# A gated recurrent scan on one core: low halves from a scan instruction, 48-column tiles in runs of 12, and block work in halves

## The reference, cut to what matters

```
xz = seq @ W_z ; xr = seq @ W_r ; xh = seq @ W          # for all steps at once
def step(h, xs):
    z  = sigmoid(xzt + h @ U_z + vz)
    r  = sigmoid(xrt + h @ U_r + vr)
    hh = tanh(xht + r * h @ U + vh)
    h_new = (1.0 - z) * h + z * hh
    return (h_new, h_new)
_, out_t = jax.lax.scan(step, h0, xs)
```

## Time and profile before

| | us |
|---|---|
| median of 3 runs | 6808.79 (6806.77 to 6811.7) |
| the profiled execution's own time | 6811.76 |
| its span | 6809.9 |
| PE busy in the span | 5998.4 (88%) |
| PEld busy | 5642.2 (83%) |
| DVE busy | 4955.6 (73%) |
| ACT busy | 3331.6 (49%) |

### The profile page before, as it was taken

How to read it: one execution, slowest core, us unless ns; L and a number is a source line. 1 busy time by engine, 2 the same in 40 slices (tenths; PEclk the granted TensorE clock), 3 DMA queues, 4 the chain that set the end, 5 groups by cost and what they waited for, 6 DMA issues and landing times.

```text
span 6809.9 us, 488240 instructions
## 1 busy us (share of the span) xinstructions
PE 5998.4 (88%) x200232; PEld 5642.2 (83%) x200232; DVE 4955.6 (73%) x43503; ACT 3331.6 (49%) x22603; POOL 3.5 (0%) x13
## 2 busy tenths in 40 slices
PE   7888888888888888888888888888888888888888
PEld 7888888888888888888888888888888888888888
DVE  5777777777777777777777777777777777777777
ACT  3444444444444444444444444444444444444444
POOL 0000000000000000000000000000000000000000
PEclk8999999999999999999999999999999999999999
DMA  2000000000000000000000000000000000000000
GB/s 84 17 18 15 18 17 18 17 17 17 18 17 18 15 18 17 18 18 15 18 17 18 17 18 15 18 17 18 17 17 17 18 17 18 15 18 18 17 18 15
DMA packets 80315, 129.97 MB, mean 19 GB/s; under 512 B 12336, under 2 KB 18480, under 8 KB 80304
## 3 DMA queue, kind: packets, MB, share of 16 engines
q1 hardware_dynamic: 80304, 129.81, 5.5%
HBM read 20.46 MB, written 8.65 MB: 4 GB/s over the span
## 4 chain that ended last, share of the span: by engine, by line
PE 71%; DVE 26%; issue 3%; SPq 0%; DMA 0%; ACT 0%; ACTq 0%; DVEq 0%
PE pair_r L252 30%; PE ps_z L252 24%; PE pair_h L252 17%; DVE pair_h L487 8%; DVE h_part L522 5%; DVE h_part L541 4%; DVE h_part L527 2%; DVE keep L523 2%; DVE zn L536 2%; DVE h_part L532 2%; PE ps_z L212 0%; DMA u_raw<-in_L_cond_U 0%; PE ps_o L212 0%; DVE u_max L424 0%; PE ps_x L224 0%
## 5 line engine op out<-in xcount | busy, mean ns | idle before, releaser
L252 PEld LDWEIGHTS pair_r<-h_part,u_part 128*128 128x128 f16 x65536 | 1845.1, 96 | 1119.9 <-DVE h_part L541 1115.8
L252 PE MATMUL pair_r<-h_part,u_part 128*128 128x32 f16 x65536 | 2048.7, 177 | 771.1 <-DVE h_part L541 758.6
L252 PE MATMUL pair_h<-rh_part,u_part 128*128 128x32 f16 x65536 | 2016.6, 177 | 12.5 <-DVE rh_part L505 12.5
L252 PE MATMUL ps_z<-h_part,u_part 128*128 128x32 f16 x65536 | 1961.5, 176 | 0.0
L252 PEld LDWEIGHTS pair_h<-rh_part,u_part 128*128 128x128 f16 x65536 | 1842.8, 96 | 17.3 <-DVE rh_part L505 15.7
L252 PEld LDWEIGHTS ps_z<-h_part,u_part 128*128 128x128 f16 x65536 | 1795.3, 95 | 0.0
L487 DVE TENSOR_REDUCE pair_r<-pair_r 128x4 f32<-128x20 f32 x4096 | 759.4, 186 | 818.1 <-PE pair_r L252 615.1
L351 ACT ACTIVATE pair_r<-pair_r 128x4 f32<-128x4 f32 x4096 | 644.8, 158 | 1445.1 <-DVE pair_r L487 1182.4
L487 DVE TENSOR_REDUCE pair_h<-pair_h 128x4 f32<-128x12 f32 x4096 | 717.7, 175 | 665.7 <-PE pair_h L252 665.7
L351 ACT ACTIVATE th_z<-ps_z 128x8 f32<-128x8 f32 x2048 | 364.1, 178 | 1046.0 <-DVE ps_z L487 1046.0
L337 ACT ACTIVATE pair_h<-xp 128x8 f32 (+1 forms) x2049 | 369.9, 181 | 807.8 <-DVE zn L536 807.8
(11 more groups left out here) (70 smaller groups left out, 3275.9 us busy)
## 6 DMA issues: line engine op xcount, KB each, us to landing
w_stage<-w_in SPq DMA_DIRECT2D x384, 256.0 KB, 2.3
x_tok<-in_x SPq DMA_DIRECT2D x68, 128.0 KB, 2.6
out_dram<-o_tok SPq DMA_DIRECT2D x66, 128.0 KB, 2.3
mlp_w<-in_L_cond_W SPq DMA_DIRECT2D x2, 1024.0 KB, 6.9
u_raw<-in_L_cond_U_r SPq DMA_DIRECT2D x1, 1024.0 KB, 5.6
u_raw<-in_L_cond_U_z SPq DMA_DIRECT2D x1, 1024.0 KB, 7.6
u_raw<-in_L_cond_U SPq DMA_DIRECT2D x1, 1024.0 KB, 10.3
w_in<-in_L_cond_W_r SPq DMA_DIRECT2D x4, 256.0 KB, 9.8
```

What stands on the lines that cost most here:

```text
L252: last = nc.tensor.matmul(bank[:, SLOT * m:SLOT * m + WIDE].rearrange("p (r n) -> p r n", n=n), u_part[:, g, part, k, gm * P:(gm + 1) * P] ...
```

## The change

1. **Low parts from a scan.** `gated_full` and `new_full` for each half are gone. The low part now comes from one `tensor_tensor_scan` over 12 places (4 channels-and-batch entries of 3 places, `STEP` = 3). In each entry the scan multiplies by the factors in the places (zero, tanh, h or z_mul) and subtracts what stands in the high part's places (-1, -1, high for r; -1, 0, high for h), so the third place is the product less its high part. The tanh results are therefore written by ACT into SBUF tiles `r_scan` and `n_scan`, h lives in `r_scan` and z_mul in `n_scan`, all with a stride of 3 elements. The low part waits for the high part (`rhi`, `nhi`). `zn` is made once, 8 wide, after the last low part, and h waits for it.
2. **Runs of 12 places.** A matmul streams 48 columns rather than 32: runs of 12 f16 places taken from `h_part` or `rh_part`, with two places of each run that matter. The reduces read columns that are 12 apart.
3. **Order on PE.** In the r group 14 matmuls rather than 12 stand ahead of the wait for half 1, so output half 0 is complete after 22 rather than 20. The h group stays at 12 and 20.
4. **Block work.** `make_out`, `make_y` and the copy to `y_cur` are each cut into two halves and put behind different turn steps; `hist` is laid out with time innermost; the output transposes move from turn step 1 to 2, the output copy from 2 to 3. The projection's store moves from DVE to ACT, as one 64-wide instruction before the tanhs of the fifth step and one behind its `hist` copy. SP issues the store of the output after the twelve weight loads of a block rather than before.
5. `seed(pair_h)` no longer waits for `zn1`. GpSimd has some more memsets at the start.

```
-    WIDE = 32
-    SLOT = WIDE + B
+    STEP, RUN, WIDE = 3, 12, 48
+    SLOT = WIDE + RUN
+    PITCH = HS * STEP + RUN - B * STEP
...
-                n = (ADDENDS[g] - 1) * B
-                moving = parts[:, k, :, :].rearrange("p a b -> p (a b)").unsqueeze(1).broadcast_to([P, WIDE // n, n])
+                n = ADDENDS[g] - 1
+                at = k // HC * n * PITCH + k % HC * B * STEP
+                runs = parts[:, at:at + n * PITCH].rearrange("p (a c) -> p a c", c=PITCH)[:, :, 0:RUN]
+                moving = runs.unsqueeze(1).broadcast_to([P, WIDE // (n * RUN), n, RUN])
...
+                ahead = 3 if g == R else 2
...
+                for m, k in first[:ahead]:
+                    product(1, m, k)
                 pe.wait_ge(s[src + "1"], t1)
...
-                        tanh(ps_r[hf][:, TANH:TANH + HS], ps_r[hf], R, HS, f"r{hf}_sum", t1, f"r{hf}_th")
+                        tanh(r_scan[:, half[hf], 1], ps_r[hf], R, HS, f"r{hf}_sum", t1, f"r{hf}_th")
...
+                def low(parts, count, hi, hf, factors, done):
+                    V.tensor_tensor_scan(part_of(parts, count, hf, hi + 1), factors[:, half[hf]].rearrange("p s c -> p (s c)"),
+                                         part_of(parts, count, hf, hi), 0.0, ALU.mult, ALU.subtract).then_inc(s[done], 1)
...
-                new_full(0)
                 keep_low()
                 new_low(0)
                 new_high(1)
-                new_full(1)
                 new_low(1)
-                V.tensor_tensor(h_cur[:, :], keep[:, :], zn[:, :], ALU.add).then_inc(s["h_ok"], 1)
+                V.tensor_tensor(zn[:, :], z_mul, n_scan[:, :, 1], ALU.mult).then_inc(s["zn_ok"], 1)
+                dve.wait_ge(s["zn_ok"], t1)
+                V.tensor_tensor(h_cur, keep[:, :], zn[:, :], ALU.add).then_inc(s["h_ok"], 1)
...
+            def store_projection(i, ring, bb):
+                return A(xp[:, i, bass.ds(ring, TB), bb], ps_p[:, bb * TB:(bb + 1) * TB], ACT.Identity,
+                         bias=v_bias[:, i, bb:bb + 1])
...
-                    if proj is not None and u == K - 1:
-                        store_projection(*proj)
-                    if turn is not None and u == 0:
-                        make_out(turn[0])
-                    if turn is not None and u == 2:
-                        dve.wait_ge(s["y_copied"], turn[1])
-                        make_y(turn[2])
+                    if turn is not None and u < 2:
+                        make_out(u, turn[0])
+                    if turn is not None and u >= 2:
+                        make_y(u - 2, turn[2], turn[1])
```

More of the change, by code:

```diff
@@ L121, in gru_kernel, with part_of, place, keep_place @@
         half = (slice(0, HS), slice(HS, S))
+        by_half = lambda a: a.rearrange("p (h s) -> p h s", h=2)
+        def part_of(parts, count, hf, part):
+            at = (hf * count + part) * PITCH
+            return parts[:, at:at + HS * STEP]
+        def place(parts, count, hf, part, step=STEP - 1):
+            return part_of(parts, count, hf, part).rearrange("p (s c) -> p s c", c=STEP)[:, :, step]
+        def keep_place(low):
+            both = h_part[:, 0:2 * 2 * PARTS * PITCH].rearrange("p (h a s c) -> p h a s c", h=2, a=2 * PARTS, c=STEP)
+            return both[:, :, KEEP + low, 0:HS, STEP - 1]
         BYTES = 16 * B
@@ L303, in steps @@
                         transpose_block(ps_x, lambda c: x_tok[:, c * P:(c + 1) * P]).then_inc(s["x_tr"], 1)
-                    if turn is not None and u == 1:
+                    if turn is not None and u == 2:
                         put_out(turn[1])
             def put_out(nb):
-                pe.wait_ge(s["o_sum"], nb)
+                pe.wait_ge(s["o_sum"], nb * 2 if isinstance(nb, int) else pe.snap(nb * 2))
                 transpose_block(ps_o, lambda c: oT[:, c * B:(c + 1) * B, :].rearrange("p b t -> p (b t)"))\
@@ L351, in tanh, with steps @@
                 A(to, bank[:, SUM:SUM + n], ACT.Tanh, scale=scale_reg[g]).then_inc(s[done], 1)
-            def steps(t0, count, ring, turn=None):
+            def store_projection(i, ring, bb):
+                return A(xp[:, i, bass.ds(ring, TB), bb], ps_p[:, bb * TB:(bb + 1) * TB], ACT.Identity,
+                         bias=v_bias[:, i, bb:bb + 1])
+            def steps(t0, count, ring, turn=None, proj=None):
                 for u in range(count):
                     t1 = act.snap(t0 + (u + 1))
+                    if proj is not None and u == K:
+                        act.wait_ge(s["proj_mm"], act.snap(proj[2] + 2))
+                        store_projection(proj[0], proj[1], 0)
                     prv = act.snap(ring + (u - 1) if u else (ring + (2 * TB - 1)) % (2 * TB))
@@ L570, in steps, with make_out @@
+            def make_out(part, ring):
+                V.scalar_tensor_tensor(oT[:, half[part], :], hist[:, half[part], bass.ds(ring, TB)], 1.0 / H_SCALE,
+                                       y_cur[:, half[part], :], ALU.mult, ALU.add).then_inc(s["o_sum"], 1)
+            def steps(t0, count, turn=None):
                 for u in range(count):
                     step(dve.snap(t0 + (u + 1)))
-                    if proj is not None and u == K - 1:
-                        store_projection(*proj)
@@ L574, in steps @@
[L574 to L579 removed]
+                    if turn is not None and u < 2:
+                        make_out(u, turn[0])
+                    if turn is not None and u >= 2:
+                        make_y(u - 2, turn[2], turn[1])
             with dve.Fori(0, NB) as n:
                 other = dve.snap(((n + 1) % 2) * TB)
[L583 removed]
+                steps(dve.snap(n * TB), TURN, turn=(other, n, dve.snap(n + 2)))
@@ L584, in _ @@
                 with dve.Fori(0, GM) as i:
-                    steps(dve.snap(n * TB + i * BODY + TURN), BODY, proj=(dve.snap(n * GM + i + 2), i, other))
+                    steps(dve.snap(n * TB + i * BODY + TURN), BODY)
             dve.wait_ge(s["copied"], 1)
-            make_out((NB - 1) % 2 * TB)
+            for part in range(2):
+                make_out(part, (NB - 1) % 2 * TB)
 _INS = ["x", "cond_1024", "L0_cond_W1", "L0_cond_b1", "L0_cond_W2", "L0_cond_b2",
```

153 lines of the change are left out of this document (73 added, 80 removed).

## The result

The changed kernel takes 6748.12 us (median of 4 runs, 6746.14 to 6750.98), against 6808.76 us for the kernel before beside it (4 runs). The ratio is 0.9911, 95% interval 0.9895 to 0.9926. It is faster by 0.9%, 61 us, where 116 us were forecast.

What follows compares the result with a forecast made beforehand. A ring through PE and DVE was taken to bound the kernel. Span 6809.9 less 72 (steps), 31 (store) and 15 (turn), plus 2, gave 6694 us, so a median of 6693; range 6630 to 6800.

Steps and rivals of the forecast that it cites:

- plain steps: Every step of the ring through PE and DVE: 0.035 us saved, 72 us over 2048 steps.
- fifth steps: Last step of a round: moving the projection's store off DVE saves a further 0.08 us, 31 us in all.
- turn: Four steps with block work: halved output block and the like save 0.46 us a block, 15 us in all.
- the r part's rival: r's chain misses its tie with z's end by 0.05 us, steps save nothing: 6765 us, chance 0.12.
- round steps all alike: Sign of being right: the five steps of a round take equal time.
- the waits of the h group on the scan of r: Sign of being wrong: new waits of PE's h group for r's scan.
- The step that failed: Late h priced only at half output blocks behind it: four cost 0.03 to 0.07 us each, 0.2 a block.
- scan and dependence save 0.042: Behind the h group: low part freed from the full product saves 0.06 us, the longer scan costs 0.018.
- all else costs 0.007: Per step: h's half 0 starts its high part 0.002 us later, and the r part's tie costs 0.005.
- half-throughput rule: DVE's built-in scan runs at half throughput: 0.021 us longer instead of 0.018, so a step gains 0.003 less.
- 0.007 for the end of the last matmul of a group: On PE, 16 more columns delay the end of a group's last matmul by 0.007 us; PE's pace is unchanged.
- The rival that 48 columns set PE's pace: Every matmul slows, at 1.5 ns each by 295 us: about 6988 us, chance 0.07.
- the rival of a dearer scan: DVE's scan takes 215 ns rather than about 180, in the h and r parts: about 6903 us, chance 0.11.

Runs made afterwards that it cites:

- zn_early: The changed kernel with zn moved ahead of the second scan of h; 6663.31 us, ratio 0.9787.
- h_late: The kernel before with one more dependent DVE instruction, a copy of zn, ahead of h; 7040.86 us, ratio 1.0343.
- h_late48: The kernel h_late with 48 columns in each matmul rather than 32; 7021.82 us, ratio 1.0325.
- pairs: The changed kernel with two rounds written out per loop pass on PE, ACT and DVE; 7842.05 us, ratio 1.1513.
- dve_pairs: The changed kernel with two rounds written out per loop pass on DVE alone; 6868.77 us, ratio 1.0102.
- no_scan: zn_early with the scan replaced by full products and four-element differences, the new layout kept; 6971.96 us, ratio 1.0242.
- wide48: The kernel before with 48 columns in each matmul rather than 32; 6831.01 us, ratio 1.0035.
- ahead3: The kernel before with 14 r matmuls rather than 12 ahead of the wait for half 1; 6827.79 us, ratio 1.0039.
- act_store: The kernel before with the projection's store moved from DVE to ACT, placed as in the change; 6791.62 us, ratio 0.9981.

## Why the prediction was half right

The sum against the measurement, in us a block (36 plain steps, 12 fifth, 12 first, 4 of the turn), each place as the difference to before:

| place | forecast | after | zn_early |
|---|---|---|---|
| plain steps | 36 x -0.035 = -1.26 | 36 x -0.046 = -1.66 | -1.70 |
| fifth steps | 12 x -0.115 = -1.38 | 12 x -0.118 = -1.42 | -1.42 |
| first steps | 12 x -0.035 = -0.42 | 12 x +0.123 = +1.48 | -0.58 |
| turn | 4 x -0.035 - 0.46 = -0.60 | -0.35 | -0.86 |
| block | -3.66 | -1.95 | -4.54 |

Times 32, the forecast is 117 us and the measurement 62, as between the spans 6809.9 and 6748.3.

The 6748 us lie within the range, but that is luck in part: the range reached so far for the sake of the r part's rival, and what used that room is a cost to which the prediction gave no term. Its own sign "round steps all alike" is the one that failed, and of its signs of being wrong the waits of the h group on the scan of r came, in the long first steps.

**The step that failed** is that of the turn: "the last scan starts at 3.28 in the step, zn at 3.38 and h, which waits for zn, at 3.57". The number is right (h at 0.35 to 0.40 behind the r group's start; 3.57 is 0.35 into the next step). But the lateness was priced only where block work stands behind h. DVE has one more thing there: at the end of each round it goes back to the head of its loop, and 0.55 us lie between h and the next reduce. Before, h started 0.19 after the r group and the loop's instructions 0.06 ahead of h, so the way back was hidden, with some 0.06 over up to the 0.74 at which the reduce is due. After, 0.39 + 0.55 is 0.94. Against the forecast that is (0.123 + 0.035) x 12 x 32 = 61 us in the rounds, and 0.25 x 32 = 8 in the turns, where the larger gain in the block work (below) made up for a part. Three sides show it: zn_early takes the lateness out of the change, h_late and h_late48 put it into the kernel before, and pairs and dve_pairs have long and usual first steps in one execution, with and without the way back. The plain steps gave back 13 us of this loss, 0.046 each instead of 0.035.

**The h stretch and the scan.** The net was right and its parts were not. Forecast: scan and dependence save 0.042, all else costs 0.007. In the new layout, no_scan puts the scan at 0.15, and the rest of the layout at 0.10. Of that, wide48 measured 0.014 for columns and ahead3 0.015 for the order. That leaves some 0.07 for the tanhs to SBUF and for operands at a stride of three elements; the order of DVE's instructions is the same in both. The rows show that each is dearer in no_scan than before: a tanh 176 ns against 158, the high part of h 165 against 153, the four-element difference 171 against 163. How much each adds to the step stays open. By the half-throughput rule that the prediction takes from the Trainium skill ("DVE: opcode table, instruction layouts, handler registers and perf-mode slots", Datapath and trigger behaviour) the scan would be 0.021 us longer than a four-element difference. The trace does not settle it: 183 ns is 0.020 more than the difference of the kernel before (L541, 163), but 0.012 more than the one in the new layout (171).

**48 columns.** The term "0.007 for the end of the last matmul of a group" came out twice as large in wide48, 0.014 us a step, 22 us in all. The rival that 48 columns set PE's pace is refuted: z's 32 loads take 0.81 us in wide48, and r's take 0.79 after the change. At 1.2 GHz they do count. The first step of the changed kernel (window: us, PE, PEld, DVE and ACT busy, clock):

```profile
75.43:79.24 3.81, 3.81 (x96) 3.81 (x97) 1.38 (x10) 1.12 (x8) 0.00 (x0) 0.50 0.02 4
```

39.7 ns a matmul against 26.6 in the earlier trace rows, the 13 forecast.

**The store.** The fifth step was right to 0.003, partly by luck: the plain part of the gain was 0.011 larger than forecast, and 0.011 of the store's effect stayed in the step. The tanhs of r were covered, as judged, though each store takes 321 ns and not 220; the late `z_keep` of act_store was not foreseen. The Trainium skill ("ScalarE: Activation LUTs", What ACT_TABLE_LOAD costs) has a line for an activation whose bias is an operand per partition, 280 ns + 0.833 a column; for 64 columns that is 333, an estimate by that page, and the trace's 321 is near it. I had priced the store from a tanh without such a bias.

**The turn and the other rivals.** The saving in the block work could have been larger than 0.46 a block: in zn_early the turn is 0.86 shorter, 0.66 of it beyond the plain gain of its four steps. In the change itself, where h is late, only 0.17 of that is left. The rival of a dearer scan did not come true: a scan takes 183 ns. "The r part eats the gain" did not come true in the steps: z to h rose by 0.03, and the r group fell by 0.04. The 6748 us lie near that rival's number all the same, by another mechanism.

## What to carry to other kernels

An instruction that becomes later costs something wherever its engine has another duty behind it: look for block work, and also for the end of each loop pass, where the way back (0.55 us here from the last instruction's start to the next one's) is hidden only as far as the engine has slack. A wait on the last instruction also holds back the loop's own instructions behind it. An independent product belongs ahead of the long dependent one: that single line was worth 85 us, more than the whole measured gain of the change. Unrolling a loop to save its way back can cost more than it saves once the code is fetched anew, in each pass (pairs) or in each block (dve_pairs).

## What the runs showed of the hardware that was not expected

- Two rounds in a pass made PE fetch 32.52 MB of code and wait 3.6 us for it 192 times; on DVE alone it cost 5 us a block.
- With the same waits, 32 columns held a mean clock of 0.912 and 48 columns one of 0.996. The kernel with wider matmuls was no slower (ratios 1.0325 and 1.0343, whose intervals overlap), although its plain steps were 0.011 us longer (3.267 against 3.256).
- In a chain the width of a group counts, though it doesn't set the pace: plus 16 columns in all groups cost 0.014 us a step, minus 24 in the h group gained 0.015.
- Reads of PSUM at 12 columns' distance cost the reduces nothing (176 and 186 ns, against 175 and 186 before).
